# Key and value stage: evictions between the halves of the norms, gathers in halves, an earlier transpose

## The reference, cut to what matters

```python
x = _layernorm(x + _L0_ffn_ref(x, ...), axis=-1)
...
def _L1_attn_ref(X, ln_w, ln_b, W_in, b_in, W_out, b_out):
    h = _layernorm(X, ln_w, ln_b)
    qkv = h @ W_in + b_in
    Q, K, V = jnp.split(qkv, 3, axis=-1)
    Q = _rope_half(Q)
    K = _rope_half(K)
    A = jnp.sum(_cos_sim(K) * V, axis=-2)
    Y = A[:, None, :] * Q
    Y = Y @ W_out + b_out
    return Y + X
```

## Time and profile before

| | us |
|---|---|
| runs | 2707.1, 2707.72, 2717.12; median 2707.72 |
| the profiled execution | 2706.93, its span from first to last instruction 2704.9 |
| busy in the span | PE 2159.2, VectorE 1936.6, ScalarE 1540.5, GpSimd 1486.3 |
| granted TensorE clock, mean | 0.885 of full speed |

### The profile page before, as it was taken

One profiled execution on the slowest core, in us unless ns is written; L12 is line 12 of the kernel. 1 busy time (PEld: TensorE's weight loads), 2 busy tenths in 40 slices (PEclk: granted clock), 3 DMA queues, 4 the chain that ended last, 5 costly groups with the idle time before them and its releaser, 6 DMA issues. The chain is left out here.

```text
span 2704.9 us, 61578 instructions
## 1 busy us (share of the span) xinstructions
PE 2159.2 (80%) x19761; PEld 1584.5 (59%) x19762; DVE 1936.6 (72%) x5279; ACT 1540.5 (57%) x3098; POOL 1486.3 (55%) x2287
## 2 busy tenths in 40 slices
PE   8947888888888878888887799784888847758887
PEld 5625555555565555565555688563444435548887
DVE  4539999999999999999999344465222257747776
ACT  5658888998999888888895122453111112212222
POOL 2437777887788777777787133342111144415444
PEclk9977888898888898888897899787999978879999
DMA  5766666665666666656664476343122233321110
GB/s 173 239 200 167 164 167 164 167 186 156 175 172 167 167 167 165 175 158 159 167 179 120 130 234 202 127 136 108 66 70 68 63 92 116 115 79 44 47 43 31
DMA packets 295365, 373.44 MB, mean 138 GB/s; under 512 B 44852, under 2 KB 234870, under 8 KB 295126
## 3 DMA queue, kind: packets, MB, share of 16 engines
q1 hardware_dynamic: 285254, 343.10, 45.5%
q0 software_dynamic: 9872, 27.28, 3.0%
HBM read 151.03 MB, written 85.00 MB: 87 GB/s over the span
## 5 line engine op out<-in xcount | busy, mean ns | idle before, releaser
L667 POOL TENSOR_TENSOR p_CR<-p_pc 128x256 f32<-128x256 f32 x512 | 373.4, 729 | 218.2 <-DVE p_pc L986 195.9
L671 POOL TENSOR_TENSOR p_BR<-p_pb 128x256 f32<-128x256 f32 x512 | 373.3, 729 | 26.0
L999 DVE TENSOR_TENSOR p_M<-p_ps_sc,p_D 128x512 f32<-128x512 f32 x512 | 327.3, 680 | 71.6 <-PE p_ps_sc L748 71.6
L748 PE MATMUL p_ps_sc<-p_CR,p_BR 64*128 64x128 f32 x4096 | 321.7, 300 | 69.0 <-DVE p_M L999 47.7
L748 PEld LDWEIGHTS p_ps_sc<-p_CR,p_BR 64*128 64x128 f32 x4096 | 272.5, 201 | 129.4 <-issue 101.1
L881 ACT ACTIVATE p_D<-p_ps_x 128x512 f32<-128x512 f32 x512 | 275.4, 589 | 80.5 <-PE p_ps_x L714 78.9
L763 PE MATMUL p_ps_y<-p_M,p_uexp 128*32 128x128 f32 x4096 | 290.8, 295 | 3.3 <-issue 2.3
L986 DVE SCALAR_TENSOR_TENSOR p_pc<-p_ps_c,p_beta,p_cs 128x256 f32<-128x256 f32 x512 | 243.1, 475 | 31.2 <-DMA p_sn<-p_tr_s 28.4
L763 PEld LDWEIGHTS p_ps_y<-p_M,p_uexp 128*32 128x32 f32 x4096 | 228.0, 118 | 46.0 <-issue 31.8
L986 DVE SCALAR_TENSOR_TENSOR p_pc<-p_ps_c,p_beta,p_sn 128x256 f32<-128x256 f32 x512 | 242.7, 474 | 0.0
L992 DVE SCALAR_TENSOR_TENSOR p_pb<-p_ps_b,p_beta,p_cs 128x256 f32<-128x256 f32 x512 | 242.6, 474 | 0.0
(11 more groups left out here) (278 smaller groups left out, 5417.1 us busy)
## 6 DMA issues: line engine op xcount, KB each, us to landing
p_cs<-p_tr_c SPq DMA_DIRECT2D x256, 256.0 KB, 4.0
p_sn<-p_tr_s SPq DMA_DIRECT2D x256, 256.0 KB, 4.5
p_phib<-scratch_phi SPq DMA_DIRECT2D x256, 128.0 KB, 3.1
p_x<-scratch_rt SPq DMA_DIRECT2D x72, 128.0 KB, 2.0
scratch_ro<-p_o POOLq DMA_DIRECT2D x72, 128.0 KB, 2.0
p_xT<-in_xT SPq DMA_DIRECT2D x64, 128.0 KB, 4.4
scratch_u<-p_u SPq DMA_DIRECT2D x16, 512.0 KB, 3.6
scratch_wu<-p_wu SPq DMA_DIRECT2D x16, 512.0 KB, 4.3
```

The costliest lines, as they stand in the source:

```text
L667: e.tensor_tensor(CR[:, p, g, :], pc[:, g % 2, 0, :], pc[:, g % 2, 1, :], ALU.add).then_inc(S["rotC"], 1)
L671: e.tensor_tensor(BR[:, p, g, :], pb[:, g % 2, 0, :], pb[:, g % 2, 1, :], ALU.add).then_inc(S["rotB"], 1)
L748: m = e.matmul(sc_ps[half][:, (g * 2 + b) * L:(g * 2 + b + 1) * L], BR[half * 64:half * 64 + 64, p, 2 * q + g, b * L:(b + 1) * L], CR[half ...
L999: e.tensor_tensor(M[:, m_slot(p, n), :], sc_ps[n % 2][:, :], D[:, n, :], ALU.mult).then_inc(S["m_ok"], 1)
```

## The change

In `key_value_product`, with SyncE's part left as it is:

- `norm_vector` gets two halves of its own, `norm_stats` (up to the variance) and `norm_out` (wait for the root, scaling). VectorE's `norm(t + 1)` becomes `sums` (the two sums and the first norm's statistics), `first_out` (first scaling, second statistics) and `second_out`. K's eviction stands between `sums` and `first_out`, V's between `first_out` and `second_out`.
- K's unrotated half is copied by ScalarE (`kc_ok`) instead of VectorE, so `kr_ok` counts two per chunk instead of four.
- ScalarE writes `hT` of the next chunk ahead of the squares of K.
- GpSimd's step t becomes: gather of t + 2 for b = 0, `kni` of t - 1, first norm's root of t + 1, gather of t + 2 for b = 1, second norm's root of t + 1.
- The loops of GpSimd, TensorE, ScalarE and VectorE are written out.

```diff
@@ -1071,6 +1071,27 @@
+
+def norm_stats(e, S, N, t, src):
+
+    at_least(e, S["ln_out"], t, 2, 0)
+    for b in range(BATCH):
+        e.bn_stats(N["st"][:, b, :], src[:, b, :]).then_inc(S["ln_stat"], 1)
+    at_least(e, S["ln_stat"], t, 2, 2)
+    e.memset(N["go"][:, :], 0.0).then_inc(S["ln_mv"], 1)
+    for b in range(BATCH):
+        e.bn_aggr(N["mv"][:, b, :], N["st"][:, b, :]).then_inc(S["ln_mv"], 1)
+    at_least(e, S["ln_mv"], t, 3, 3)
+    e.tensor_scalar(N["ve"][:, :], N["mv"][:, :, 1], EPS_LN, None, ALU.add).then_inc(S["ln_var"], 1)
+
+
+def norm_out(e, S, N, t, src, dst):
+
+    at_least(e, S["ln_rs"], t, 1, 1)
     for b in range(BATCH):
         e.tensor_scalar(dst[:, b, :], src[:, b, :], N["mv"][:, b, 0:1], N["rs"][:, b:b + 1], ALU.subtract, ALU.mult
                         ).then_inc(S["ln_out"], 1)
...
@@ -2026,35 +2047,39 @@
-            def gather(t, p):
-                counted(e, S["prep"], S["slot_in"][p], t - p, 8, 16)
-                counted(e, S["prep"], S["s2_ok"], t, 1, -1)
-                for b in range(BATCH):
-                    for n in range(2):
-                        e.indirect_dma_start(got[:, p, b, n, :], None, W["ro"].rearrange("j p d -> (j p) d"),
-                                             bass.IndirectOffsetOnAxis(ap=slot[:, p, 2 * b + n:2 * b + n + 1], axis=0)
-                                             ).then_inc(S["got"][p], 16)
-
-            def step(t, p, late=False, last=False):
-                if not last:
-                    norm_pool(e, S2, N2, t + 1, mhalf)
-                    norm_pool(e, S, N, t + 1, mhalf)
-                if not late:
-                    gather(t + 2, p)
+            def gather(t, p, b):
+                if b == 0:
+                    counted(e, S["prep"], S["slot_in"][p], t - p, 8, 16)
+                    counted(e, S["prep"], S["s2_ok"], t, 1, -1)
+                for n in range(2):
+                    e.indirect_dma_start(got[:, p, b, n, :], None, W["ro"].rearrange("j p d -> (j p) d"),
+                                         bass.IndirectOffsetOnAxis(ap=slot[:, p, 2 * b + n:2 * b + n + 1], axis=0)
+                                         ).then_inc(S["got"][p], 16)
+
+            def key_norm(t):
                 at_least(e, S["kk_ok"], t, 2, 2)
                 at_least(e, S["A_mm"], t, 1, 0)
                 e.tensor_tensor(kni[:, :], kn[:, :], mhalf[:, :], ALU.pow).then_inc(S["kn_ok"], 1)
-            gather(0, 0)
-            gather(1, 1)
+
+            def step(t, p):
+                if t + 2 < NC:
+                    gather(t + 2, p, 0)
+                if t:
+                    key_norm(t - 1)
+                if t + 1 < NC:
+                    norm_pool(e, S2, N2, t + 1, mhalf)
+                if t + 2 < NC:
+                    gather(t + 2, p, 1)
+                if t + 1 < NC:
+                    norm_pool(e, S, N, t + 1, mhalf)
+            for t in range(2):
+                for b in range(BATCH):
+                    gather(t, t, b)
             norm_pool(e, S2, N2, 0, mhalf)
             norm_pool(e, S, N, 0, mhalf)
-            step(0, 0)
-            step(1, 1)
-            with e.Fori(1, NC // 2 - 1) as j:
-                step(j * 2, 0)
-                step(j * 2 + 1, 1)
-            step(NC - 2, 0, True)
-            step(NC - 1, 1, True, True)
+            for t in range(NC):
+                step(t, t % 2)
+            key_norm(NC - 1)
 
@@ -2105,13 +2130,8 @@
-            step(0, 0)
-            step(1, 1)
-            with e.Fori(1, NC // 2 - 1) as j:
-                step(j * 2, 0)
-                step(j * 2 + 1, 1)
-            step(NC - 2, 0)
-            step(NC - 1, 1, True)
+            for t in range(NC):
+                step(t, t % 2, t == NC - 1)
...
@@ -2125,35 +2145,36 @@
-            def step(t, p, last=False):
+            def step(t, p):
+                at_least(e, S["kb_ok"], t, 2, 2)
+                at_least(e, S["kv_ok"], t, 2, 0)
+                at_least(e, S["kk_ok"], t, 2, 0)
+                for b in range(BATCH):
+                    e.activation(kr[:, b, P:DM], kb[:, b, 2 * P:3 * P], ACT.Copy).then_inc(S["kc_ok"], 1)
                 at_least(e, S["q_mm"], t, 1, 1)
                 at_least(e, S["q_rot"], t, 2, 0)
-                if not (isinstance(t, int) and t < 2):
+                if t >= 2:
                     at_least(e, S["stored"][p], t - p, 8, 0)
                 for n in range(3):
                     e.activation(q[:, n, :] if n < 2 else qo[:, p, 1, :], q_ps[n // 2][:, n % 2 * CT:(n % 2 + 1) * CT],
                                  ACT.Identity, bias=bq[:, n:n + 1]).then_inc(S["q_ok"], 1)
-                at_least(e, S["kr_ok"], t, 4, 4)
+                if t + 1 < NC:
+                    turned(t + 1)
+                at_least(e, S["kr_ok"], t, 2, 2)
+                at_least(e, S["kc_ok"], t, 2, 2)
                 at_least(e, S["kn_ok"], t, 1, 0)
                 for b in range(BATCH):
                     at_least(e, S["kk_ok"], t, 2, b)
                     e.activation(kk[:, :], kr[:, b, :], ACT.Square, accum_out=kn[:, b:b + 1]).then_inc(S["kk_ok"], 1)
-                if not last:
-                    turned(t + 1)
             turned(0)
-            step(0, 0)
...
+            for t in range(NC):
+                step(t, t % 2)
-            def norm(t, p):
+            def sums(t, p):
                 at_least(e, S["x_in"][p], t - p, 8, 16)
                 at_least(e, S["got"][p], t - p, 32, 64)
                 at_least(e, S["s2_ok"], t, 1, 0)
...
                 e.tensor_tensor(s2[:, :, :], s1[:, :, :], got[:, p, :, 1, :], ALU.add).then_inc(S["s2_ok"], 1)
                 at_least(e, S["s2_ok"], t, 1, 1)
-
-                def kept():
-                    if not (isinstance(t, int) and t < 2):
-                        at_least(e, S["x2_out"][p], t - p, 8, 0)
-                    at_least(e, S["ln_out"], t, 2, -2)
-                norm_vector(e, S2, N2, t, s2, x2[:, p, :, :], kept)
+                norm_stats(e, S2, N2, t, s2)
+
+            def first_out(t, p):
+                if t >= 2:
+                    at_least(e, S["x2_out"][p], t - p, 8, 0)
+                at_least(e, S["ln_out"], t, 2, -2)
+                norm_out(e, S2, N2, t, s2, x2[:, p, :, :])
                 at_least(e, S["bln_out"], t, 2, 2)
-
-                def free():
-                    at_least(e, S["hn_tr"], t, 1, 0)
-                norm_vector(e, S, N, t, x2[:, p, :, :], hn, free)
+                norm_stats(e, S, N, t, x2[:, p, :, :])
+
+            def second_out(t, p):
+                at_least(e, S["hn_tr"], t, 1, 0)
+                norm_out(e, S, N, t, x2[:, p, :, :], hn)
 
...
-            def step(t, p, last=False):
-                if not last:
-                    norm(t + 1, 1 - p)
+            def step(t, p):
+                more = t + 1 < NC
+                if more:
+                    sums(t + 1, 1 - p)
                 for b in range(BATCH):
                     at_least(e, S["k_mm"], t, 2, b + 1)
                     at_least(e, S["k_rot"], t, 4, 0)
-                    at_least(e, S["kr_ok"], t, 4, 0)
+                    at_least(e, S["kc_ok"], t, 2, 0)
                     e.tensor_tensor(kb[:, b, :], k_ps[b][:, 0:3 * P], bk[:, :], ALU.add).then_inc(S["kb_ok"], 1)
+                if more:
+                    first_out(t + 1, 1 - p)
                 at_least(e, S["v_mm"], t, 1, 1)
                 at_least(e, S["kv_ok"], t, 2, 0)
                 for b in range(BATCH):
                     e.tensor_tensor(vb[:, b, :], v_ps[:, b * DM:(b + 1) * DM], bv[:, :], ALU.add).then_inc(S["vb_ok"], 1)
+                if more:
+                    second_out(t + 1, 1 - p)
                 at_least(e, S["kb_ok"], t, 2, 2)
                 at_least(e, S["rope_in"][p], t - p, 16, 32)
                 for b in range(BATCH):
@@ -2200,8 +2228,8 @@
                 at_least(e, S["kk_ok"], t, 2, 0)
                 for b in range(BATCH):
                     e.tensor_tensor(kr[:, b, 0:P], kt[:, 0, b, :], kt[:, 1, b, :], ALU.add).then_inc(S["kr_ok"], 1)
-                    e.tensor_copy(kr[:, b, P:DM], kb[:, b, 2 * P:3 * P]).then_inc(S["kr_ok"], 1)
-                at_least(e, S["kr_ok"], t, 4, 4)
+                at_least(e, S["kr_ok"], t, 2, 2)
+                at_least(e, S["kc_ok"], t, 2, 2)
                 at_least(e, S["vb_ok"], t, 2, 2)
                 at_least(e, S["A_mm"], t, 1, 0)
                 for b in range(BATCH):
...
-            norm(0, 0)
-            step(0, 0)
-            step(1, 1)
-            with e.Fori(1, NC // 2 - 1) as j:
-                step(j * 2, 0)
-                step(j * 2 + 1, 1)
-            step(NC - 2, 0)
-            step(NC - 1, 1, True)
+            sums(0, 0)
+            first_out(0, 0)
+            second_out(0, 0)
+            for t in range(NC):
+                step(t, t % 2)
             add_up(NC - 1)
```

(6 more changed lines are left out.)

## The result

The changed kernel takes 2760.7 us (median of 4 runs, 2758.5 to 2762.8) against 2707.4 us: 1.9% slower, ratio 1.0192 with a 95% interval of 1.0163 to 1.0221. The profiled execution took 2758.5 us, its span is 2756.8. The forecast was slower, 2742 with a range to 2757, so the sign was right and the time lies 3.7 us above the range.

What follows compares the result with a forecast made beforehand. VectorE's own order was taken to set the 13.53 us step, with two GpSimd round trips and a gather wait. Thirteen steps 2.7 longer (35), ends -1: +34 on 2706.93 gives 2741, forecast 2742, range 2730 to 2756 (also 2729 to 2757).

Steps and rivals of the forecast that it cites:

- The ring of slot store, slot load and GpSimd's queue: First gather waits for indices loaded behind q's store, delaying GpSimd's roots and VectorE: steps 16.25 instead of 13.53 us, 35 more.
- Covered by 1.7: TensorE's sum_up and q with ScalarE's evictions end at 13.3 us, ahead of the q rotation at some 15.0.
- The ends of the stage: First step and last two steps, outside the thirteen with the slot wait: together about -1 us.
- Step 0: Slots are early, but VectorE's first_out stands behind the first k product, not covered there: +0.9 us.
- Step 14: Gathers nothing, so no slot wait: some 11.6 us against 13.36, -1.8.
- Step 15: TensorE's chain at the stage's end, starting 0.2 us earlier.
- (a): Rival: no slot wait, TensorE and ScalarE bound in 12.1 us a step; 20 less, 2687 us; 5%.
- (b): Rival: same loop much shorter, idle GpSimd's gathers going out faster, step at most 14.6 us; 2718 us; 6%.
- (c): Rival: longer loop, slot load landing in 3.6 us instead of 2.2, 18 more; 2760 us; 9%.
- Loops: Writing out the four engines' loops: taken as 0, with 2 us either way for the longer code.
- second gather pair: GpSimd's two gathers beside VectorE's first_out: 0 lost; by the skill's port rule it could be 8 us more.

Runs made afterwards that it cites:

- q_ahead_of_sum: The changed kernel with TensorE's q products ahead of sum_up of the chunk before; 2748.4 us, 1.0134 of before.
- slots_at_start: The changed kernel with all 16 chunks' row indices loaded by one DMA at the start of the stage; 2671.1 us, 0.9869 of before.
- slot_before_stores: The changed kernel with SyncE issuing chunk t+3's row indices ahead of chunk t's x2 and q stores, its loop written out; 2735.3 us, 1.0105 of before.

## Why the prediction was wrong in size and right in kind

*The ring of slot store, slot load and GpSimd's queue: right.* Its steps against the changed kernel's step from 2314.14: slot issued at 2.09 (2.08 for this parity); first gather at 5.07 (4.8); first root done at 8.76 (8.7); first scaling at 8.90 (8.8); second scaling at 12.08 (12.1); the kv products at 2328.32, 14.18 (12.1 + 0.7 + 0.92 + 0.5 = 14.2). The load still lands 2.2 after its issue (median), so between landing and gather some 0.8 passed rather than 0.3; the pairs of gathers gave 0.1 each back, 2.28 and 2.3 instead of 2.4. Over the thirteen steps the first gather starts 4.7 to 6.0 us behind the step's end, 5.19 in the mean, so this term was 0.4 too small.

*"Covered by 1.7": the step that failed.* I had TensorE's `sum_up` and q end in time, at 0.95 and 2.84 us. These are durations from a trace in which nothing held TensorE up in front of them. The change's own wait, the key root at 8.0, lets TensorE run dry first, and then both take the lower clock: 1.87 and 4.68. That is 2.8 us more, of which 1.7 were covered, so VectorE should wait about 1.1; it waited 0.83 in this step, 11.2 us in the thirteen steps and 13.0 over the stage. I had asked what a lower clock would do to k and found it harmless; for q, which the same paragraph calls covered by 1.7, I didn't ask. Measured steps are 17.27 on average ((2436.58 - 2212.02) / 13) against 16.25, which makes 13.3 us, and `q_ahead_of_sum` brings them back to 16.26.

*The ends of the stage.* Step 0: +1.9 against +0.9, as k took 5.49 us there, 4.41 before. Step 14: 11.29 against 11.6. Step 15: 9.2 against 12.3 before, where I had -0.2: its k ran at full clock, 2.85 instead of 4.54, and began 1.4 us ahead of the step's end, where it had begun at the end before. With 13 x (17.27 - 13.53) = 48.7, this adds up: 1.9 + 48.7 - 2.1 - 3.1 = 45.4, the growth of the stage. The forecast was 34. The remaining 6.5 of the profiled pair, and about 8 of the two medians (53.3 - 45.4), come from outside the stage; no experiment ties them to the change, and their cause stays open; single executions of the kernel before alone lie up to 26 us apart. They matter for the range: 45.4 instead of 34 in the stage alone would have given some 2753, inside it. The missed wait for q made the forecast too low, but only with the 8 us on top does the time pass 2757 (the prediction names the range twice, as 2730 to 2756 and as 2729 to 2757).

*The rivals.* (a), the change without the wait, didn't come, and its price was low: with the indices at the start it is 2671 and not 2687, for the same reason, a k of 4.54 us taken over from the trace of before. (b) and (c): a longer ring did come, but mostly by TensorE's clock; the slot load landed in the 2.2 us assumed.

*Loops, second gather pair.* Nothing, as forecast: the gather beside the first scaling took 1.01 to 1.02 us in every step read. Here the rule of the Trainium skill (SBUF — State Buffer, Who interferes with whom), under which it could be held up by a VectorE operation with the second port, isn't borne out by these rows, as in the prediction. They don't refute it either: the scaling takes 0.41 us for 128x256, no less than an addition or product of two tensors of that size (0.42), so nothing shows that it used the second port.

The clock itself, in rows: 0.87 in before's steps with 3.4 us of idle TensorE in front of k and k at 4.54 us, 1.00 with 1.1 us idle and k at 2.85, 0.80 in the changed kernel with 3.9 us idle in front of `sum_up`. Half of 2.4 GHz is 1.2, and 1.87 against 0.95 is such a half. The gap right in front of a product doesn't settle it: behind a gap of 1.1 us k took 2.85 in most steps of `slots_at_start`, 4.54 in two of them, and 4.3 to 5.5 in `q_ahead_of_sum`, where TensorE had also sat idle for 3.1 to 3.7 us ahead of the transposes before it.

## What to carry to other kernels

Before an instruction is moved up in a queue, look at when its own input is *issued*, not only whether it had arrived at the old place: these row indices were never waited for until GpSimd came for them before they had been issued, and then all that stood behind the wait, on three engines, went with it. When a change adds a wait in front of matrix products, cost those that follow at the lower clock, and cost those that it brings closer together at the higher one; a margin of 1.7 us on products of 3.8 is none. And a slower kernel can hold most of a faster one: one load moved to the start of the stage turned +1.9% into -1.3%.

## What the runs showed of the hardware

- Behind idle stretches of 3.6 to 4.8 us TensorE's products took the lower clock in all thirteen steps of the changed kernel: in the step shown 1.87 against 0.95 us for `sum_up` and 4.68 against 2.84 for q, with a mean granted clock of 0.80 over the step against 1.00 in most steps of `slots_at_start`. A wait thus costs more than its own length.
- Shorter gaps can cost it too: in `slot_before_stores` TensorE was idle for 2.0 to 2.6 us in front of `sum_up` in twelve of the steps, and q took 4.3 to 5.5 us.
- From the issue of a 2 KB load on SyncE's queue to the gather that waits for it 2.5 to 3.7 us passed in the changed kernel (median 2.95), of which the landing is 2.2.
